# First graph aggregation on one core: the 500-column one-hot of the hot tiles moves from ACT to VectorE, and four products of a tile become one

## The chip, the core and the metric

The kernel runs on one core of a Trainium2 chip. The time is that of the device, in microseconds, from the start of one execution to its end. It is given as the median of a few executions. Beside the times there is one profiled execution, in which the hardware profiler recorded the instructions of each engine: PE (the matrix engine), DVE (VectorE), ACT (ScalarE), POOL (GpSimd) and SP (SyncE).

## The reference

A graph of 3125 nodes with 256 features and 50,000 weighted edges goes through two layers, each an aggregation over the graph and a mixture of experts. Only the first aggregation is touched here:

```python
h = layernorm(x) @ W
msgs = h[dst] * edge_weight[:, None]
x = x + segment_sum(msgs, src, 3125) + bias
```

`dst` is sorted and its values are drawn as 3125 u^2 with u uniform, so that low nodes are frequent: 500 of the 3125 nodes, the "hot" ones, receive about four tenths of the edges. All in float32.

## The kernel before

**Preparation** (`stage_prepare`, L534). The nodes are cut into 25 blocks of P = 125. Each edge gets a bucket: the block of its source, and 25 more buckets for edges whose target is hot (`dst` < HOT * P = 500, L660). The edges are put into tiles of 128 slots, tile by tile of one bucket, in `pg.slots` [128, EDGE_PAD, 4] with EDGE_PAD = 592 tiles; the last dimension holds source place in its block, weight and target, so a column of one field is strided by four floats. One part of the edges goes there by POOL's scatters to DRAM (L634), the rest by products with permutation matrices (`Permute`, L417); `unpack` (L516) and `merge` (L523, L526 to L528) end the preparation on VectorE by adding the two parts. `step` is a `Chain` (L138): VectorE waits for each such instruction before it issues the next. A `pg.block()` ends when all engines are done, so the aggregation cannot start before the last step.

**Cold tiles** (class `Aggregate`, L748). A round is 16 tiles. ACT copies the targets as integers and the keys of four tiles (`stage`, L776, L782 and L783), POOL gathers 128 rows of `h` for each tile from DRAM by an indirect DMA (`gather_round`, L801) into one of 16 places of `G`, VectorE writes the weighted one-hot of the source place, 125 columns, into `S` (`onehot`, L840), and PE multiplies two tiles into one bank (`product_four`, L826 in this stage), which VectorE adds to the rows of `pg.X` of the source block (`add`, L859). POOL may gather into a place again when PE is done with the tile of the round before.

**Hot tiles** (`stage_aggregate_nodes`, L881). Their targets are among 500 nodes, so no row is gathered: the stage builds the matrix `pg.A` [125, 4, 3125], weights by hot target (row in its block of 125, block d of four) and source node, and later multiplies it with the 500 hot rows of `h` (L1069; the three later feature layers use the same `pg.A` at L1099). A round is HR = 12 tiles, in Q = 3 quads of QUAD = 4 tiles of one source block. For each tile VectorE writes the weighted one-hot of the source place, `S`, 125 columns (`sources`, L940). ACT writes the one-hot of the target, `T`, 500 columns, with two activations: `away` = |column - target| (L926), then relu(1 - away) (L932); its keys come from `stage_hot` (L916, L917). PE makes, for each of the four target blocks d, the product of `T[:, k, d * P:(d + 1) * P]` and `S[:, k, :]`, summed over the quad's four tiles (`quad_product`, L950), and VectorE adds the bank of 500 columns to `pg.A` (`quad_add`, L960) and writes the sources of the quad's places for the next round.

**The order.** While both lists last (`both_lists`), each engine has an order written out by hand: PE takes four cold tiles, then three times a quad and four cold tiles; ACT stages four cold tiles between the targets of two quads; VectorE adds a four, adds a quad and writes the next sources. POOL's queue in this stage holds nothing but the gathers. In this run there are 16 cold rounds (256 gathers) and 17 hot ones (204 tiles, 51 quads). Before the loop VectorE writes 8 cold and 12 hot one-hots (L865, L1027), adds the bias to X (L1028) and clears `pg.A` (L1030); the first hot product waits for that (`s_add`). After the loop SP loads the hot rows (L1083) in a new block.

Of the kernel before, what the change touches and what calls it, by code (L numbers as in the profile page):

```python
# [24 lines left out]
ALU = mybir.AluOpType  # L25
ACT = mybir.ActivationFunctionType
# [4 lines left out]
P = 125  # L31
# [8 lines left out]
HOT = 4  # L40
QUAD = 4
HR = 3 * QUAD
# [6 lines left out]
EDGE_PAD = -(-(EDGE_TILES + 2 * HR) // ROUND) * ROUND  # L49
# [22 lines left out]
class Program:  # L72
# [8 lines left out]
    def sb(self, name, shape, dt=fp32, ctx=None):  # L81
        return (ctx or self.ctx).enter_context(self.nc.sbuf_tensor(name, shape, dt))
# [451 lines left out]
def stage_prepare(pg, x, src, dst, edge_weight, w_l0, bias_l0):  # L534
    nc = pg.nc
    with ExitStack() as ctx:
        sb = lambda n, s, d=fp32: pg.sb(n, s, d, ctx)
# [17 lines left out]
        perm = Permute(pg, ctx, sort_room)  # L555
# [18 lines left out]
        with pg.block() as block:  # L574
# [64 lines left out]
            def _(dve):  # L639
                step = Chain(dve, s_ch)  # L640
                v = nc.vector
# [57 lines left out]
                first, end = buf["start"][0:1, NT:NT + 1], buf["start"][0:1, EB:EB + 1]  # L699
# [13 lines left out]
                perm.unpack(step)  # L713
                dve.wait_ge(s_back, 16)
                perm.merge(step)

            @block.tensor
            def _(pe):
# [162 lines left out]
def stage_aggregate_nodes(pg):  # L881


    nc = pg.nc
    SPAN = 4
    Q = HR // QUAD
    with ExitStack() as ctx:
        agg = Aggregate(pg, ctx, "agg0", "node", pg.X)
        sb = lambda n, s, d=fp32: pg.sb(n, s, d, ctx)
        S, T = sb("hot_sources", [128, HR, P]), sb("hot_targets", [128, HR, HOT * P])  # L890
        away = sb("hot_away", [128, QUAD, HOT * P])
        key = sb("hot_key", [128, HR, 3])
        s_key, s_neg, s_away, s_src, s_dst, s_mm, s_add, s_bias = (pg.sem(f"hot_{n}", ctx) for n in (
            "key", "negated", "away", "sources", "targets", "mm", "add", "biased"))
# [14 lines left out]
        def block_psum(q):  # L909
            return pg.ps[0:P, 4 + q, 0:HOT * P].rearrange("p (d q) -> p d q", d=HOT)  # L910

        def stage_hot(act, first, i):

            act.wait_ge(s_src, i * HR + HR)
            act.wait_ge(s_dst, i * HR + HR)
            nc.scalar.copy(key[:, :, 0:2], pg.slots[:, pg.tiles_at(first + i * HR, HR), 0:2]).then_inc(s_key, 1)  # L916
            nc.scalar.activation(key[:, :, 2], pg.slots[:, pg.tiles_at(first + i * HR, HR), 2],  # L917
                                 ACT.Copy, scale=-1.0).then_inc(s_neg, 1)

        def targets(act, i, q):  # L920

            act.wait_ge(s_neg, i + 1)
            for u in range(QUAD):
                k = q * QUAD + u
                act.wait_ge(s_dst, i * HR + (k + HR - QUAD + 1))
                nc.scalar.activation(away[:, u, :], pg.hot_col[:], ACT.Abs,  # L926
                                     bias=key[:, k, 2:3]).then_inc(s_away, 1)
            act.wait_ge(s_mm, i * Q + (q + 1))
            for u in range(QUAD):
                k = q * QUAD + u  # L930
                act.wait_ge(s_away, i * HR + (k + 1))
                nc.scalar.activation(T[:, k, :], away[:, u, :], ACT.Relu, bias=pg.ones[:, 0:1],  # L932
                                     scale=-1.0).then_inc(s_dst, 1)

        def sources(dve, i, q):
            if q == 0:
                dve.wait_ge(s_key, i + 1)
            dve.wait_ge(s_mm, i * Q + (q + 1))
            for k in range(q * QUAD, (q + 1) * QUAD):
                nc.vector.tensor_scalar(S[:, k, :], pg.col[:, 0:P], key[:, k, 0:1], key[:, k, 1:2],  # L940
                                        ALU.is_equal, ALU.mult).then_inc(s_src, 1)

        def quad_product(pe, i, q):
            pe.wait_ge(s_add, i * Q + (q + 1))
            pe.wait_ge(s_src, i * HR + (HR + (q + 1) * QUAD))
            pe.wait_ge(s_dst, i * HR + (HR + (q + 1) * QUAD))
            for d in range(HOT):
                for u in range(QUAD):
                    k = q * QUAD + u
                    last = nc.tensor.matmul(block_psum(q)[:, d, :], T[:, k, d * P:(d + 1) * P], S[:, k, :],  # L950
                                            start=(u == 0), stop=(u == QUAD - 1))
            last.then_inc(s_mm, 1)

        def quad_add(dve, first, i, q):
# [8 lines left out]
        with pg.block() as block:  # L963
            @block.scalar
            def _(act):
                n, m, first = agg.rounds(act), agg.rounds(act, HOTTER), agg.rounds(act, FIRST)
                act.sem_inc(s_dst, HR)

                def both_lists(i):
                    agg.stage(act, i, 0)  # L970
                    stage_hot(act, first, i)
                    for q in range(Q):
                        agg.stage(act, i, q + 1)
                        targets(act, i, q)

                def either_list(i):


                    with act.If(n > i - 1):
                        agg.stage(act, i, 0)  # L980
                    with act.If(m > i - 1):
                        stage_hot(act, first, i)
                    with act.If(n > i - 1):
                        agg.stage(act, i, 1)
                    with act.If(n > i):
                        agg.stage(act, i, 2)
                        agg.stage(act, i, 3)
                    with act.If(m > i):
                        for q in range(Q):
                            targets(act, i, q)  # L990

                rounds_of_lists(act, both_lists, either_list)
# [987 lines left out]
def build(nc, x, src, dst, edge_weight, L0_gnn_W, L0_gnn_bias, L0_ffn_router_w, L0_ffn_w1, L0_ffn_b1,  # L1980
          L0_ffn_w2, L0_ffn_b2, L1_gnn_W_in, L1_gnn_b_in, L1_gnn_W1, L1_gnn_b1, L1_gnn_g1, L1_gnn_be1,
          L1_gnn_W2, L1_gnn_b2, L1_gnn_g_out, L1_gnn_b_out, L1_ffn_Wr, L1_ffn_W1s, L1_ffn_b1s,
          L1_ffn_W2s, L1_ffn_b2s, L1_ffn_W1p, L1_ffn_b1p, L1_ffn_W2p, L1_ffn_b2p, out):
    with ExitStack() as ctx:
        pg = Program(nc, ctx)
        pg.ps = ctx.enter_context(nc.psum_tensor("ps", [128, 8, 512], fp32))
        pg.X = pg.sb("X", [P, NT, D])
        pg.stats = pg.sb("stats", [P, NT, 6])
        pg.col = pg.sb("col", [128, 128])
        pg.part = pg.sb("part", [128, 1])  # L1990
        pg.moe_tiles = pg.sb("moe_tiles", [1, MOE_TILES])
        pg.ident = pg.sb("ident", [128, 128])
        pg.tri = pg.sb("tri", [128, 128])
        pg.ones = pg.sb("ones", [128, 128])
        pg.prio = pg.sb("prio", [P, NX])
        pg.token = pg.sb("token", [P, TOP * NT])
        pg.H = nc.dram_tensor("h_rows", [N, D], fp32).ap()
        pg.pay_dram = nc.dram_tensor("payloads", [128 * EDGE_PAD, 4], fp32).ap()
        pg.Y = nc.dram_tensor("expert_out", [MOE_TILES * SLOT, D], fp32).ap()

        edges = ctx.enter_context(ExitStack())
        pg.slots = pg.sb("slots", [128, EDGE_PAD, 4], ctx=edges)
        pg.owner_t = pg.sb("owner_t", [1, EDGE_PAIRS], int32, ctx=edges)
        pg.owner_n = pg.sb("owner_n", [1, EDGE_PAIRS], int32, ctx=edges)
        pg.owner_h = pg.sb("owner_h", [1, EDGE_PAIRS], int32, ctx=edges)
        pg.lists = pg.sb("lists", [1, 6], int32, ctx=edges)
        pg.tiles = pg.sb("tiles", [1, EDGE_PAIRS], ctx=edges)
        pg.bias_l0 = pg.sb("bias_l0", [P, D], ctx=edges)
        pg.hot_col = pg.sb("hot_col", [128, HOT * P], ctx=edges)
        stage_prepare(pg, x, src, dst, edge_weight, L0_gnn_W, L0_gnn_bias)  # L2010
        pg.A = pg.sb("A_hot", [P, HOT, N], ctx=edges)
        stage_aggregate_nodes(pg)
        with ExitStack() as c1:
            Mixture(pg, c1, "moe0", lambda k: L0_ffn_router_w.rearrange("e (k p) -> k p e", p=128)[k],
                    L0_ffn_w1, L0_ffn_b1, L0_ffn_w2, L0_ffn_b2).run()
        stage_network(pg, L1_gnn_W_in, L1_gnn_b_in, L1_gnn_W1, L1_gnn_b1, L1_gnn_g1, L1_gnn_be1,
                      L1_gnn_W2, L1_gnn_b2, L1_gnn_g_out, L1_gnn_b_out)
        edges.close()

        with ExitStack() as c1:  # L2020
            Mixture(pg, c1, "moe1", lambda k: L1_ffn_Wr[k * 128:(k + 1) * 128, :],
                    L1_ffn_W1p, L1_ffn_b1p, L1_ffn_W2p, L1_ffn_b2p,
                    shared=(L1_ffn_W1s, L1_ffn_b1s, L1_ffn_W2s, L1_ffn_b2s), out=out).run()
# [30 lines left out]
```

## Time and profile before

| | us |
|---|---|
| median of 3 executions | 3124.06 (3123.24 to 3125.66) |
| the profiled execution | 3120.67 |
| its span in the profile | 3118.9 |
| PE busy | 2358.3 (76% of the span) |
| POOL busy | 1466.8 (47%) |
| DVE busy | 1362.2 (44%) |
| ACT busy | 947.9 (30%) |
| first aggregation's loop, first to last hot instruction | 437.5 to 789.5 |

Busy times are shares of the whole span, over stages with different limits; matmuls are pipelined, so a busy PE is not PE at its peak. An engine's idle time is put down to what released it: "ACT agg_key L783" is the semaphore of that line, "issue" is time in which it waited for nothing that the profile shows. A group's count and busy time belong to the instructions of one line, and its mean is that of one instruction from start to end, which is more than the step between two that overlap.

### The profile page before, as it was taken

How to read it: one execution, taken by the hardware profiler on the slowest of the kernel's cores; microseconds unless marked ns; L12 is line 12 of the kernel's file. 1: busy time of each engine (PE TensorE's matmuls, PEld its weight loads, DVE VectorE, ACT ScalarE, POOL GpSimd, SP SyncE). 2: the span in 40 equal slices, each digit the busy share in tenths (PEclk: the TensorE clock that was granted, in tenths of full speed). 3: DMA queues.
4: the chain of work that ended last, by engine and by line, in shares of the span. 5: the costliest groups of instructions: out<-in, count | busy, mean ns of one | idle time of the engine just before them, and what ended most of it. 6: DMA issues, size and time to landing. Idle time of an engine off the chain costs nothing. (4 is left out here: it accounts for less than half of the span.)

```text
span 3118.9 us, 52528 instructions
## 1 busy us (share of the span) xinstructions
PE 2358.3 (76%) x13838; PEld 2087.4 (67%) x13838; DVE 1362.2 (44%) x3807; ACT 947.9 (30%) x2741; POOL 1466.8 (47%) x1443
## 2 busy tenths in 40 slices
PE   1989959999769615667575676656665799999999
PEld 0789959888668503666535665436564499999988
DVE  6789976666344352434333434234343541111122
ACT  4268858788012101000040000220000433333332
POOL 1388867776004452777606777227776001111152
PEclk9889979999859857888787888778987879999999
DMA  2100013333019732333303333123333049999932
GB/s 78 35 4 3 3 47 100 104 104 93 21 65 322 242 86 76 105 104 104 90 23 108 104 104 105 36 80 104 104 105 86 11 128 308 326 329 325 326 94 64
DMA packets 250553, 363.11 MB, mean 116 GB/s; under 512 B 64305, under 2 KB 195854, under 8 KB 250054
## 3 DMA queue, kind: packets, MB, share of 16 engines
q0 software_dynamic: 73728, 163.66, 19.3%
q1 hardware_dynamic: 173460, 194.84, 19.1%
q10 hardware_dynamic: 3250, 3.20, 0.3%
q8 instruction: 58, 0.95, 0.1%
q14 instruction: 57, 0.47, 0.0%
HBM read 322.19 MB, written 38.64 MB: 116 GB/s over the span
## 5 line engine op out<-in xcount | busy, mean ns | idle before, releaser
L801 POOL DMA_INDIRECT z_or_xn<-h_rows,agg_idx x768 | 730.3, 951 | 524.5 <-ACT agg_key L783 301.2
L832 PE MATMUL ps<-z_or_xn 128*128 128x125 f32 x3072 | 496.1, 328 | 325.0 <-DMA z_or_xn<-h_rows,agg_idx 281.2
L832 PEld LDWEIGHTS ps<-z_or_xn 128*128 128x128 f32 x3072 | 461.5, 237 | 363.9 <-issue 284.9
L1410 POOL DMA_INDIRECT moe_room<-h_rows,moe_inverse x112 | 105.8, 944 | 725.4 <-PE ps L1491 390.4
L859 DVE TENSOR_TENSOR z<-z,ps 128x250 f32 x384 | 159.3, 415 | 543.7 <-PE ps L832 510.3
L782 ACT CAST agg_idx<-slots 128x4 int32 x264 | 51.8, 196 | 1056.2 <-PE ps L832 605.9
L634 POOL DMA_INDIRECT payloads<-pay_st,idx_st x176 | 247.7, 1407 | 159.7 <-DMA idx_st<-slot_i 106.3
L801 POOL DMA_INDIRECT agg_room<-h_rows,agg_idx x256 | 249.1, 973 | 97.6 <-issue 70.2
L1610 ACT ACTIVATE moe_room<-ps,moe_b 128x128 f32<-128x128 f32 x560 | 163.6, 367 | 364.0 <-PE ps L1503 363.9
L502 PE MATMUL ps<-perm_tile,perm_weighted 125*128 125x296 f32 x1792 | 247.5, 301 | 9.7 <-ACT perm_weighted L489 9.7
L502 PEld LDWEIGHTS ps<-perm_tile,perm_weighted 125*128 125x128 f32 x1792 | 247.2, 190 | 10.6 <-ACT perm_weighted L489 10.6
L840 DVE TENSOR_SCALAR z_or_xn<-col,agg_key 128x125 f32<-128x125 f32 x792 | 241.1, 367 | 19.9 <-ACT agg_key L783 19.9
L489 ACT ACTIVATE perm_weighted<-oh_or_permute 125x128 fp32r<-125x128 f32 x672 | 206.1, 390 | 111.3 <-DVE oh_or_permute L473 111.2
L1636 DVE TENSOR_TENSOR moe_room<-ps,moe_b 128x256 f32<-128x256 f32 x112 | 47.5, 424 | 431.1 <-PE ps L1515 431.1
L1099 PE MATMUL ps<-A_hot,agg_hot_rows 125*128 (+1 forms) x624 | 174.1, 434 | 61.7 <-DMA agg_hot_rows<-h_rows 61.7
L950 PEld LDWEIGHTS ps<-hot_sources,hot_targets 128*125 128x125 f32 x1632 | 189.9, 192 | 18.4 <-issue 15.2
L950 PE MATMUL ps<-hot_sources,hot_targets 128*125 128x125 f32 x1632 | 189.9, 275 | 14.1 <-DVE A_hot L1030 13.6
L1099 PEld LDWEIGHTS ps<-A_hot,agg_hot_rows 125*128 125x128 f32 x624 | 139.6, 244 | 79.5 <-DMA agg_hot_rows<-h_rows 62.6
L1503 PE MATMUL ps<-moe_room,moe_w_ring 128*128 128x128 f32 x1520 | 185.6, 278 | 2.8 <-issue 2.0
L1503 PEld LDWEIGHTS ps<-moe_room,moe_w_ring 128*128 128x128 f32 x1520 | 177.5, 193 | 6.5 <-issue 4.1
L1515 PE MATMUL ps<-moe_w_ring,moe_room 128*128 128x256 f32 x760 | 177.2, 380 | 2.7 <-issue 2.7
L1420 POOL DMA_INDIRECT moe_room<-expert_out,moe_slot_i x100 | 120.8, 1208 | 94.7 <-DMA expert_out<-moe_room 58.3
(272 smaller groups left out, 3572.2 us busy)
## 6 DMA issues: line engine op xcount, KB each, us to landing
moe_w_ring<-in_L_ffn_W1p_dram SPq DMA_DIRECT2D x38, 1024.0 KB, 7.0
moe_w_ring<-in_L_ffn_W2p_dram SPq DMA_DIRECT2D x38, 1024.0 KB, 7.9
moe_w_ring<-in_L_ffn_w_dram SPq DMA_DIRECT2D x76, 256.0 KB, 5.0
moe_room<-in_L_ffn_W1p_dram SPq DMA_DIRECT2D x18, 1024.0 KB, 7.1
moe_room<-in_L_ffn_W2p_dram SPq DMA_DIRECT2D x18, 1024.0 KB, 7.7
expert_out<-moe_room SPq DMA_DIRECT2D x112, 128.0 KB, 5.7
z_or_xn<-h_rows,agg_idx POOLq DMA_INDIRECT x768, 2.7
moe_room<-in_L_ffn_w_dram SPq DMA_DIRECT2D x36, 256.0 KB, 4.7
```

Source lines behind the costliest of these rows:

```text
L489: last = self.pg.nc.scalar.activation(self.weighted[:, u, x, :], self.place[:, u, :], ACT.Copy, scale=self.parts[:, bass.ds(i * long + c, ...
L502: last = nc.tensor.matmul(self.ps[:, x // 2, h, :], self.weighted[:, u, x, :], self.tile[:, u, h * (EDGE_PAD // 2):(h + 1) * (EDGE_PAD // 2)],
L634: g.indirect_dma_start(pg.pay_dram, bass.IndirectOffsetOnAxis(ap=idx_st[:, h, k:k + 1], axis=0), pay_st[:, h, k, :], None).then_inc(scat[8 ...
L801: self.pg.nc.gpsimd.indirect_dma_start(self.G[:, k, :], None, self.pg.H, bass.IndirectOffsetOnAxis(ap=self.idx[:, k:k + 1], axis=0)).then_ ...
L832: last = nc.tensor.matmul(out[:, c, :], self.G[:, k, c * 128:(c + 1) * 128], self.S[:, k, :], start=(u == 0), stop=(u == PAIR - 1))
L840: self.pg.nc.vector.tensor_scalar(self.S[:, k, :], self.pg.col[:, 0:P], self.key[:, k, 0:1], self.key[:, k, 1:2], ALU.is_equal, ALU.mult). ...
L859: nc.vector.tensor_tensor(a, a, p, ALU.add).then_inc(self.s_acc, 1)
L950: last = nc.tensor.matmul(block_psum(q)[:, d, :], T[:, k, d * P:(d + 1) * P], S[:, k, :], start=(u == 0), stop=(u == QUAD - 1))
L1099: last = nc.tensor.matmul(pg.ps[:, 4 + c, 0:width], Hh[:, d, c * 128:(c + 1) * 128], pg.A[:, d, bass.ds(first, width)], start=(d == 0), st ...
L1503: last = nc.tensor.matmul(self.fc1_psum(t, f), w[:, k, f * 128:(f + 1) * 128], self.xt[:, t % self.RT, k, :], start=(k == 0), stop=(k == K ...
L1515: last = nc.tensor.matmul(ps[:, 6 + t % 2, 0:D], self.hid[:, t % self.RH, f, :], w[:, f, :], start=(f == 0), stop=(f == FK - 1))
L1610: last = a.activation(self.hid[:, t % self.RH, f, :], self.fc1_psum(t, f), ACT.Gelu, bias=self.b1_sb[:, bass.ds(e, 1), f])
```

## The change

The two one-hots swap their widths. VectorE's weighted one-hot now spans 500 columns, target block and source place together, and stands as the moving operand; ACT's one-hot of the target's row in its block has 125 columns and is the weight. One product a tile gives the whole bank of 500 columns. For this the keys of all tiles are worked out once, behind `merge`: `pg.hot_key[:, :, 1]` is the target's row in its block, `pg.hot_key[:, :, 0]` the source place plus 125 times the block. `row_of` and `block_of` count minus 125 for each block's start that the target has reached.

```diff
@@ stage_prepare, VectorE, behind perm.merge(step)
+                block_of, dst_of = perm.got_i[:, 0, :], pg.slots[:, :, 2]
+                key_of, row_of = pg.hot_key[:, :, 0], pg.hot_key[:, :, 1]
+                step(v.tensor_scalar(row_of, dst_of, float(P), -float(P), ALU.is_ge, ALU.mult))
+                for d in range(2, HOT):
+                    step(v.tensor_scalar(block_of, dst_of, float(d * P), -float(P), ALU.is_ge, ALU.mult))
+                    step(v.tensor_tensor(row_of, row_of, block_of, ALU.add))
+                step(v.tensor_tensor(key_of, pg.slots[:, :, 0], row_of, ALU.subtract))
+                step(v.tensor_tensor(row_of, dst_of, row_of, ALU.add))
@@ stage_aggregate_nodes
-        S, T = sb("hot_sources", [128, HR, P]), sb("hot_targets", [128, HR, HOT * P])
-        away = sb("hot_away", [128, QUAD, HOT * P])
+        S, T = sb("hot_sources", [128, HR, HOT * P]), sb("hot_targets", [128, HR, P])
+        away = sb("hot_away", [128, QUAD, P])
@@ stage_hot, ACT
-            nc.scalar.copy(key[:, :, 0:2], pg.slots[:, pg.tiles_at(first + i * HR, HR), 0:2]).then_inc(s_key, 1)
-            nc.scalar.activation(key[:, :, 2], pg.slots[:, pg.tiles_at(first + i * HR, HR), 2],
+            nc.scalar.copy(key[:, :, 1], pg.slots[:, pg.tiles_at(first + i * HR, HR), 1])
+            nc.scalar.copy(key[:, :, 0], pg.hot_key[:, pg.tiles_at(first + i * HR, HR), 0]).then_inc(s_key, 1)
+            nc.scalar.activation(key[:, :, 2], pg.hot_key[:, pg.tiles_at(first + i * HR, HR), 1],
                                  ACT.Copy, scale=-1.0).then_inc(s_neg, 1)
@@ targets, ACT
-                nc.scalar.activation(away[:, u, :], pg.hot_col[:], ACT.Abs,
+                nc.scalar.activation(away[:, u, :], pg.col[:, 0:P], ACT.Abs,
@@ sources, VectorE
-                nc.vector.tensor_scalar(S[:, k, :], pg.col[:, 0:P], key[:, k, 0:1], key[:, k, 1:2],
+                nc.vector.tensor_scalar(S[:, k, :], pg.hot_col[:], key[:, k, 0:1], key[:, k, 1:2],
@@ quad_product, PE
-            for d in range(HOT):
-                for u in range(QUAD):
-                    k = q * QUAD + u
-                    last = nc.tensor.matmul(block_psum(q)[:, d, :], T[:, k, d * P:(d + 1) * P], S[:, k, :],
-                                            start=(u == 0), stop=(u == QUAD - 1))
+            for u in range(QUAD):
+                k = q * QUAD + u
+                last = nc.tensor.matmul(pg.ps[0:P, 4 + q, 0:HOT * P], T[:, k, :], S[:, k, :],
+                                        start=(u == 0), stop=(u == QUAD - 1))
@@ build
+        pg.hot_key = pg.sb("hot_keys", [128, EDGE_PAD, 2], ctx=edges)
```

## Rows read from the trace of the kernel before

**Rows 1.** Busy time by stretch: PE, PEld, DVE, ACT, POOL, granted clock, DMA share, GB/s.

```profile
463.00:470.00 7.00, 7.00 (x43) 6.78 (x43) 1.91 (x7) 0.00 (x0) 4.80 (x5) 0.76 0.34 100
503.30:769.20 265.90, 246.44 (x1747) 228.82 (x1746) 168.90 (x531) 218.21 (x464) 201.48 (x212) 0.97 0.36 104
520.00:540.00 20.00, 20.00 (x150) 18.95 (x149) 14.58 (x46) 18.59 (x39) 15.13 (x17) 1.00 0.36 105
```

**Rows 2.** Groups, 503.3 to 769.2 (the last row: whole span); columns as on the page.

```profile
L801 POOL DMA_INDIRECT agg_room<-h_rows,agg_idx x212 | 201.5, 950 | 64.8 <-issue 57.0 <-ACT agg_key L783 6.7 <-PE ps L826 1.1
...
L826 PE MATMUL ps<-agg_room 128*125 128x256 f32 x435 | 109.1, 397 | 19.5 <-DMA agg_room<-h_rows,agg_idx 16.1 <-DVE X L859 2.2 <-DVE agg_room L840 1.1
...
L960 DVE TENSOR_TENSOR A_hot<-A_hot,ps 125x500 f32 x51 | 34.5, 676 | 20.4 <-issue 15.3 <-PE ps L950 4.8
```

**Rows 3.** Groups, POOL, 1230 to 1520 (a feature layer).

```profile
L801 POOL DMA_INDIRECT z_or_xn<-h_rows,agg_idx x232 | 220.9, 952 | 70.7 <-issue 67.0 <-ACT agg_key L783 3.7
```

**Rows 4.** Timeline, POOL: start, us, line, what, [idle before and its releaser].

```profile
438.39 1.06 POOL L801 DMA_INDIRECT agg_room<-h_rows,agg_idx  x1 [15.92 <-ACT agg_key L783]
...
439.76 1.02 POOL L801 DMA_INDIRECT agg_room<-h_rows,agg_idx  x1 [0.30 <-issue]
...
443.61 6.62 POOL L801 DMA_INDIRECT agg_room<-h_rows,agg_idx  x1 [0.30 <-ACT agg_key L783]
...
471.25 0.95 POOL L801 DMA_INDIRECT agg_room<-h_rows,agg_idx  x1 [2.21 <-ACT agg_key L783]
```

**Rows 5.** Timeline, 439 to 468, DVE and PE.

```profile
439.53 3.14 DVE L940 TENSOR_SCALAR hot_sources<-col,hot_key 128x125 f32<-128x125 f32 x12
...
442.59 6.81 DVE L1028 TENSOR_TENSOR X<-X,bias_l 125x6400 f32<-125x6400 f32 x1
...
451.95 10.47 DVE L1030 MEMSET A_hot<- 125x12500 f32 x1 [2.56 <-issue]
...
462.67 5.48 PE L950 MATMUL ps<-hot_sources,hot_targets 128*125 128x125 f32 x32 [13.62 <-DVE A_hot L1030]
```

**Rows 6.** Groups, POOL, 471.2 to 503.3.

```profile
L801 POOL DMA_INDIRECT agg_room<-h_rows,agg_idx x24 | 22.8, 948 | 11.1 <-issue 7.8 <-ACT agg_key L783 3.3
```

**Rows 7.** Timeline, ACT: half a quad's activations of 500 columns, and four of 128.

```profile
603.44 2.52 ACT L926 ACTIVATE hot_away<-hot_col,hot_key 128x500 f32<-128x500 f32 x4
...
2601.94 1.14 ACT L1610 ACTIVATE moe_room<-ps,moe_b 128x128 f32<-128x128 f32 x4 [0.45 <-PE ps L1503]
```

**Rows 8.** Timeline, PE: a dense layer from 1175.54 on, the tail's three quads.

```profile
1175.54 16.64 PE L1790 MATMUL ps<-h_features,gnn_w 128*128 128x500 f32 x43
...
776.97 10.71 PE L950 MATMUL ps<-hot_sources,hot_targets 128*125 128x125 f32 x96 [0.49 <-ACT hot_targets L932]
```

**Rows 9.** Timeline, DVE, end of the preparation (merge).

```profile
429.30 1.21 DVE L526 TENSOR_TENSOR slots<-slots,oh_or_permute 128x592 f32<-128x592 f32 x1 [1.44 <-DMA slots<-payloads]
...
431.78 1.23 DVE L528 TENSOR_TENSOR slots<-slots,oh_or_permute 128x592 f32<-128x592 f32 x1
```

**Rows 10.** One line each: count, shortest/median/longest ns, first and last start, shape.

```profile
L652 DVE TENSOR_SCALAR slot_i<-src_f x1: 368/368/368, 10.6 to 10.6; 125x400 int32<-125x400 f32 x1
...
L660 DVE TENSOR_SCALAR row_f<-pay x1: 511/511/511, 14.5 to 14.5; 125x400 f32<-125x400 f32 x1
```

**Rows 11.** The same view: one-hot, two-operation tensor_scalar, wide tensor_scalar.

```profile
L840 DVE TENSOR_SCALAR agg_room<-col,agg_key x264: 330/341/549, 437.5 to 777.2; 128x125 f32<-128x125 f32 x132
...
L1703 DVE TENSOR_SCALAR moe_xn<-X,moe_mean,moe_rstd x50: 398/405/412, 852.6 to 2500.2; 125x256 f32<-125x256 f32 x50
...
L475 DVE TENSOR_SCALAR perm_tile<-tile_row,slot_f x224: 512/523/865, 176.2 to 420.9; 125x592 fp32r<-125x592 f32 x112
```

**Rows 12.** L634: before the permutation (one line), beside it (group).

```profile
L634 POOL DMA_INDIRECT payloads<-pay_st,idx_st x14: 1172/1177/4312, 121.4 to 144.0; - x14
...
L634 POOL DMA_INDIRECT payloads<-pay_st,idx_st x154 | 205.0, 1331 | 46.9 <-issue 46.9
```

**Rows 13.** The line L801, whole span.

```profile
L801 POOL DMA_INDIRECT agg_room<-h_rows,agg_idx x256: 940/946/6615, 438.4 to 768.2; - x128
```

## The prediction

> **What bounds the kernel now.** I looked first at busy times by stretch [rows 1]. In the first aggregation, between 503 and 769 us, no engine is full: PE is busy 246.4 of 265.9 us, ACT 218.2, POOL 201.5, DVE 168.9. So the waits must tell, and I took the groups of that stretch [rows 2]. POOL issues 212 gathers there (L801), 950 ns each, with 64.8 us idle before them, 0.306 us each: 212 x 1.256 = 266 us is the whole stretch. Is that 0.30 a wait for ACT's keys, which the row partly names? The same gather in a feature layer, where no hot tile is built, comes at the same step: 232 in (220.9 + 70.7) us, 1.257 each [rows 3]. So the step is POOL's own, and POOL is the loop's clock: a round is 16 gathers, 20 us. PE (L826) stops 16.1 us for gathers to land [rows 2]. ACT, the engine that the change relieves most, is busy 18.6 of 20 us [rows 1], yet behind POOL.
>
> Only the beginning is different. POOL stops before the gather at 471.25 (idle 2.21) [rows 4]: the first hot product must wait until DVE has cleared A_hot, at 451.95 + 10.47 us, so that PE resumes at 462.67 [rows 5]. From there to 503 us POOL is idle 11.1 us before 24 gathers [rows 6], 3.9 more than 24 x 0.30. In this catch-up ACT needs 2 x 2.52 us for the eight activations of a quad of hot tiles, and its key copies on top [rows 7]; four gathers take 5.0, so POOL meets ACT and PE at their own pace.
>
> **The change, part by part.** The sum is made against the profiled execution, 3120.67 us with a span of 3118.9; that lies 3.4 us under the median 3124.06, and I add the sum to the median.
>
> *ACT.* A quad's eight activations of 500 columns (four in 2.52 us) become eight of 125; four of 128 columns take 1.14 us [rows 7]. ACT saves 2.7 us a quad, some 138 us over 51 quads, and gains one key copy a round. By itself this is worth nothing: POOL's step hides it. It pays where ACT ends last, in the catch-up and by 0.5 us at the tail.
>
> *PE.* A quad is 32 matmul instructions now (the trace lists two to an fp32 product); the tail's three quads, 96 of them, take 10.71 us, 3.6 a quad. After, it is 8 of 500 columns. 43 instructions of a dense layer, nearly all 500 wide, took 16.64 us, 0.39 apart, so 0.42 for the wide ones [rows 8]: 3.4 a quad. That saves 0.2, again behind POOL. PE will stand longer for gathers, so its clock may dip more often: after the stop of 13.62 us before 462.67 the granted clock of the next 7 us was 0.76 of full [rows 1], a mean of the levels 1.2 and 2.4 GHz, and the quad took 5.48 [rows 5], 1.9 more. I cost such dips at nothing, since PE's waits for gathers cover them; without that cover one a round would be 1.9 x 16 = 30 us.
>
> *Seven new VectorE steps.* They stand at the very end of the preparation, chained behind merge (L526 to L528). DVE is done at 431.78 + 1.23 = 433.0 [rows 9], and POOL, idle for 15.92 us, starts its first gather 5.4 us later [rows 4]. Nothing lies beside them: all of it is on the path. Four are tensor_tensor on strided operands like the three of merge, whose step is (431.78 - 429.30) / 2 = 1.24 us with the gap: 5.0. Three are tensor_scalar: striding cost L660 0.14 over L652 for 400 columns [rows 10], so 0.21 for 592, on top of 0.52 for 592 contiguous ones (L475 [rows 11]): 0.73 each, 2.2. Sum **+7.2**. Below, contiguous prices: 0.52 three times and 0.80 four times (L960's 676 ns for 500 columns [rows 2]), 4.8. Above: 1.24 seven times, 8.7. I take the strided rows, since the new operands are strided.
>
> *VectorE's one-hot, 125 to 500 columns.* No row has this shape. The same two-operation form takes 341 ns at 125 columns and 405 at 256, 0.49 ns a column; the one-operation form takes 523 at 592 [rows 11]. So about 0.52, **0.18 more each**. Ahead of the loop twelve stand in front of the bias add and the clearing of A_hot (3.14 us [rows 5]), on the path to the restart at 471.25: **+2.2**, up to 3.3 if each is held up by another 0.09, as one-hots reach 549 where the median is 341. In the loop DVE gains 2.2 us on 12.7 a round; POOL's 20 covers it.
>
> *Catch-up.* ACT's quad halves, PE's shrinks by 0.2: **-1.0** of the 3.9 (0 to -2.1; the rest belongs to the restart itself).
>
> *POOL's gathers beside a wider VectorE instruction.* This decides the size. That the two hinder each other stands in the start: the gather at 443.61 took 6.62 us while the bias add ran to 449.4, and the one at 439.76, amid twelve one-hots, took 1.02 [rows 4, 5]. The nearest rows for wide instructions are the scatters L634: 1177 ns median before the permutation, 1331 mean beside it [rows 12], +154 ns, where DVE runs one instruction of 592 and two of 128 columns every 1.08 us or so. If a gather waits out the rest of the running instruction, the cost goes with the sum of squared widths per us: in the permutation 354 thousand, in the loop now 28 x 125^2 / 20 = 22 thousand, after (16 x 125^2 + 12 x 500^2) / 20 = 162 thousand. That predicts 154 x 22/354 = 10 ns for today; measured are a mean of 950 [rows 2] over a shortest of 940 [rows 13], so the form holds. After: 71, 61 more. Against the median of 946 today's loss is only 4 ns, which scales to 29, 25 more. I take the middle, 43 ns x 236 gathers from 471 us on: **+10.1**. Below: 0 (POOL slips between; nothing in the change could speed a gather). Above: 61 x 236 = 14.4.
>
> The Trainium skill, "SBUF — State Buffer", § Who interferes with whom, speaks against this change: a VectorE instruction in a 2-port mode, which it says a tensor_scalar can enter, holds a port pair that GpSimd shares for its whole length, and whichever comes second is fully blocked. The scatters' 154 ns agree that a running neighbour costs time; what the rule would make of four such instructions in a row is rival 3.
>
> *Tail.* After the last cold product PE has three quads and 0.49 us of waiting for ACT [rows 8]: -0.49 and 3 x -0.2. The four one-hots behind the last add, which nobody reads, still hold the block's end: 4 x 0.18 = +0.7. Sum **-0.4**.
>
> All: 7.2 + 2.2 - 1.0 + 10.1 - 0.4 = **+18.1**: 3138.8 for the profiled execution, **3142.2** by the median.
>
> **The rivals.** (1) *ACT paces the loop.* For it: ACT's 18.6 of 20 us, and its key copies named as releaser before L801. Against it: 1.257 us a gather where ACT has next to nothing to do [rows 3]. If the 0.30 us before each gather were ACT's, the round would fall to PE's 246.4 / 265.9 x 20 = 18.5 us: 16 x 1.5 = 24 less, against 8.0 more outside the loop: 3108. It decides if a round gets shorter than 20 us. Chance 0.05. (2) *POOL is not disturbed* and the new steps are at their low price: 4.8 + 2.2 - 2.1 - 0.4 = +4.5, 3129; L801 stays at 950 ns. Chance 0.12. (3) *A quad's four one-hots shut POOL out as one*: 4 x 0.46 = 1.8 us, a mean wait of 0.9, 48 times: +43 in place of 10.1, 3175. Against it: twelve one-hots without a gap lengthened a gather to no more than 1.02 [rows 4, 5]. Chance 0.04. (4) *The wide one-hot runs at the price of the 500-column add*, 676 ns [rows 2]: +0.34 each, 4.0 at the start and 1.3 at the tail, and POOL perhaps left alone: 7.2 + 4.0 - 1.0 + 0.2 = +10.4, 3134. DVE would be at 16.7 of 20 us, still no bound. Chance 0.07.
>
> **How the numbers follow.** Forecast 0.72, rivals 0.05, 0.12, 0.04, 0.07. A measurement of this kernel tells about 0.2% from no change, 6.2 us, so slower means over 3130.3: rivals 3 and 4 and nearly all of the forecast, 0.82. Rival 2 and a low forecast are the same, 0.13. Faster is rival 1, 0.05. Lowest sum 4.8 + 2.2 - 2.1 + 0 - 0.4 = +4.5; highest 8.7 + 3.3 + 0 + 14.4 + 0 = +26.4. So the range is 3128 to 3151; rivals 1 and 3 stay outside.
>
> **What would show it.** Right: seven DVE instructions behind L528 of some 7 us together, and the first gather later by as much; one-hots of about 0.52 us in hot_sources; ACT about half busy in the loop; PE waiting more for gathers; L801 near 0.99 us with 0.30 before it, so a round above 20 us. Wrong: L801 still at 0.95 (rival 2), a round under 20 us (rival 1), gathers of 1.5 us and more at each quad (rival 3), one-hots of 0.65 us and more (rival 4).

## The result, and the profile after

The changed kernel takes **3142.01 us** (median of 4 runs, 3137.07 to 3145.01) against 3123.76 (3123.24 to 3125.66) beside it: ratio **1.0056**, 95% interval 1.0038 to 1.0073. That is slower, as forecast, and 0.2 us from the forecast time. The profiled execution took 3137.07 us with a span of 3135.2; the span of before is 3118.9, so 16.3 us are to be found in the trace.

First the timeline of after (start, us, engine, line, what, [idle before and its releaser]): VectorE at the end of the preparation and at the loop's start, POOL's first gathers, ACT in the loop, and PE and VectorE at the tail.

```profile
432.66 0.70 DVE L718 TENSOR_SCALAR hot_keys<-slots 128x592 f32<-128x592 f32 x1
433.39 0.68 DVE L720 TENSOR_SCALAR oh_or_permute<-slots 128x592 int32<-128x592 f32 x1
434.11 0.78 DVE L721 TENSOR_TENSOR hot_keys<-hot_keys,oh_or_permute 128x592 f32<-128x592 f32 x1
...
437.70 1.22 DVE L723 TENSOR_TENSOR hot_keys<-slots,hot_keys 128x592 f32<-128x592 f32 x1
...
445.45 5.48 DVE L949 TENSOR_SCALAR hot_sources<-hot_col,hot_key 128x500 f32<-128x500 f32 x12
450.85 6.81 DVE L1036 TENSOR_TENSOR X<-X,bias_l 125x6400 f32<-125x6400 f32 x1
460.21 10.47 DVE L1038 MEMSET A_hot<- 125x12500 f32 x1 [2.55 <-issue]
...
444.31 1.06 POOL L809 DMA_INDIRECT agg_room<-h_rows,agg_idx  x1 [22.22 <-ACT agg_key L791]
445.68 12.83 POOL L809 DMA_INDIRECT agg_room<-h_rows,agg_idx  x1 [0.30 <-issue]
458.81 0.94 POOL L809 DMA_INDIRECT agg_room<-h_rows,agg_idx  x1 [0.30 <-issue]
...
481.35 1.23 POOL L809 DMA_INDIRECT agg_room<-h_rows,agg_idx  x1 [0.30 <-issue]
...
606.46 1.26 ACT L935 ACTIVATE hot_away<-col,hot_key 128x125 f32<-128x125 f32 x4
607.63 1.25 ACT L941 ACTIVATE hot_targets<-hot_away,ones 128x125 f32<-128x125 f32 x4
...
783.99 3.52 PE L958 MATMUL ps<-hot_sources,hot_targets 128*125 128x500 f32 x8
...
791.37 10.30 PE L958 MATMUL ps<-hot_sources,hot_targets 128*125 128x500 f32 x24 [0.48 <-issue]
817.46 7.87 PE L1077 MATMUL ps<-hot_rows,A_hot 125*125 125x256 f32 x28 [15.79 <-DMA hot_rows<-h_rows]
...
802.40 1.88 DVE L949 TENSOR_SCALAR hot_sources<-hot_col,hot_key 128x500 f32<-128x500 f32 x4
```

Against [rows 4, 5, 7 to 9]: the seven steps run from 432.66 to 438.92, 6.26 us, and the first gather starts 5.92 later than before (merge itself began 0.35 earlier here). The second gather is the new thing: it takes 12.83 us, from inside the twelve one-hots until just after the bias add has ended at 450.85 + 6.81 = 457.66. In the kernel before, the one long gather was the fifth, 6.62 us beside the bias add. So late is POOL afterwards that A_hot is ready when the 21st gather is due: it starts at 481.35 without a stop, where before had 2.21 us of idle time at 471.25. An activation quad takes 2.5 us in place of 5.0.

Then the loop: busy time of 20 us (PE, PEld, DVE, ACT, POOL, granted clock, DMA share, GB/s), and two groups of the stretch 509.6 to 783.3, the last 214 gathers.

```profile
520.00:540.00 20.00, 18.32 (x59) 10.65 (x58) 15.75 (x42) 9.26 (x37) 15.16 (x16) 1.00 0.36 104
```

```profile
L809 POOL DMA_INDIRECT agg_room<-h_rows,agg_idx x214 | 209.6, 979 | 65.2 <-issue 60.6 <-ACT agg_key L791 4.6
...
L834 PE MATMUL ps<-agg_room 128*125 128x256 f32 x429 | 110.6, 404 | 30.3 <-DMA agg_room<-h_rows,agg_idx 28.2 <-DVE agg_room L848 2.0
```

Beside [rows 1, 2]: ACT falls from 18.59 us to 9.26, PE from 20.00 to 18.32, DVE rises from 14.58 to 15.75. A gather's mean goes from 950 ns to 979 with the same 0.305 us before it, so the round is longer, and PE waits for gathers 28.2 us where it waited 16.1. The same by line (count, shortest/median/longest ns, first and last start):

```profile
L809 POOL DMA_INDIRECT agg_room<-h_rows,agg_idx x256: 942/946/12831, 444.3 to 783.0; - x128
...
L949 DVE TENSOR_SCALAR hot_sources<-hot_col,hot_key x216: 520/534/767, 445.4 to 803.8; 128x500 f32<-128x500 f32 x108
```

The median gather is still 946 ns [rows 13]. The mean moved because 21 gathers behind the start took 1.14 to 1.24 us and about as many 1.02; of those behind the start, none took over 1.06 before. One of the 21, with the one-hot that was running when it started:

```profile
520.69 0.52 DVE L949 TENSOR_SCALAR hot_sources<-hot_col,hot_key 128x500 f32<-128x500 f32 x1
520.83 1.20 POOL L809 DMA_INDIRECT agg_room<-h_rows,agg_idx  x1 [0.30 <-issue]
```

The one-hot ends at 521.21, the gather at 522.03, 0.82 us later. So it is with all 21: each starts 0.12 to 0.21 us after a one-hot has started and ends 0.81 to 0.82 us after that one-hot's end, just as in the kernel before the 6.62 us gather ended 0.82 us after the bias add. An undisturbed gather takes 0.95 us in all. But not every neighbour costs time: of 73 gathers behind the start that started while a one-hot was running, 25 took less than 0.96 us.

A ledger for what follows, worked out from the starts and lengths of the 256 gathers in the trace: 255 gaps of 1.25 us (0.95 and 0.30) is the shortest way from the first gather's start to the last's. What lies above that is lost, either in long gathers among the first eight, in gathers from the ninth on, or in POOL's idle time above 0.30 us. The parts count from a median gather of 946 ns and add up to the sum within 0.2 us.

| profiled execution | lost, us | first eight | later gathers | idle | mean from the ninth on, ns |
|---|---|---|---|---|---|
| before | 11.1 | 5.9 | 1.0 | 4.1 | 950 |
| after | 19.9 | 12.0 | 7.8 | 0.1 | 978 |
| keys_alone | 11.1 | 5.9 | 0.9 | 4.3 | 950 |
| wide_alone | 21.9 | 12.0 | 10.0 | 0.1 | 986 |
| halves | 15.1 | 7.4 | 2.3 | 5.4 | 955 |
| psum_col (long gather is the ninth) | 14.1 | 0.1 | 7.0 | 6.9 | 974 |
| after_again | 22.2 | 12.0 | 10.0 | 0.2 | 986 |
| bias_later_after | 14.4 | 5.3 | 9.2 | 0.1 | 983 |
| bias_later_before | 3.9 | 0.2 | 0.8 | 2.9 | 949 |
| bias_later_psum | 7.1 | 0.2 | 0.7 | 6.2 | 949 |
| clear_first_before | 15.3 | 13.1 | 2.1 | 0.2 | 954 |
| clear_first_after | 23.7 | 13.9 | 9.7 | 0.2 | 985 |
| clear_first_halves | 17.0 | 13.2 | 3.6 | 0.2 | 961 |

For the span of after: 5.9 later first gather, 8.9 more to the last gather (338.69 from the first gather's start to the last's, where before took 329.81), 0.0 at the tail (21.3 us from the last gather's start to VectorE's end in both), 14.8 in all. The other 1.5 us come later, where no instruction is changed, and are spread; runs of this kernel differ by up to 7.9.

### The profile page after: what moved, and what is told of

The parts are those of the page before. It is cut to its first block and busy times, and to the rows that moved or that the text cites. A ratio compares the mean times of both kernels' runs of the same rounds, so it can differ in the third digit from the quotient of the medians.

```text
span 3135.2 us, 50123 instructions
## 1 busy us (share of the span) xinstructions
PE 2352.4 (75%) x12614; PEld 1976.4 (63%) x12614; DVE 1414.3 (45%) x3814; ACT 821.5 (26%) x2759; POOL 1478.8 (47%) x1443
## 5 line engine op out<-in xcount | busy, mean ns | idle before, releaser
L634 POOL DMA_INDIRECT payloads<-pay_st,idx_st x176 | 247.4, 1405 | 159.6 <-DMA idx_st<-slot_i 106.3
L809 POOL DMA_INDIRECT agg_room<-h_rows,agg_idx x256 | 262.0, 1023 | 99.9 <-issue 72.5
L848 DVE TENSOR_SCALAR z_or_xn<-col,agg_key 128x125 f32<-128x125 f32 x792 | 240.8, 365 | 20.1 <-ACT agg_key L791 19.9
L958 PE MATMUL ps<-hot_sources,hot_targets 128*125 128x500 f32 x408 | 184.7, 597 | 4.7 <-DVE A_hot L1038 4.2
L834 PE MATMUL ps<-agg_room 128*125 128x256 f32 x512 | 131.8, 404 | 70.1 <-DMA agg_room<-h_rows,agg_idx 68.0
L834 PEld LDWEIGHTS ps<-agg_room 128*125 128x125 f32 x512 | 98.7, 198 | 114.8 <-issue 96.0
```

Source lines behind the costliest of these rows:

```text
L634: g.indirect_dma_start(pg.pay_dram, bass.IndirectOffsetOnAxis(ap=idx_st[:, h, k:k + 1], axis=0), pay_st[:, h, k, :], None).then_inc(scat[8 ...
L809: self.pg.nc.gpsimd.indirect_dma_start(self.G[:, k, :], None, self.pg.H, bass.IndirectOffsetOnAxis(ap=self.idx[:, k:k + 1], axis=0)).then_ ...
L834: last = nc.tensor.matmul(out, self.S[:, k, :], self.G[:, k, :], start=(u == 0), stop=(u == PAIR - 1))
L848: self.pg.nc.vector.tensor_scalar(self.S[:, k, :], self.pg.col[:, 0:P], self.key[:, k, 0:1], self.key[:, k, 1:2], ALU.is_equal, ALU.mult). ...
L958: last = nc.tensor.matmul(pg.ps[0:P, 4 + q, 0:HOT * P], T[:, k, :], S[:, k, :], start=(u == 0), stop=(u == QUAD - 1))
```

## The experiments

**Which parts make the 18 us?** My theory: the seven steps cost some 6 us, and the rest is the wide one-hot, which holds gathers up, at the start and in the loop. Its rival: the new order on ACT and PE matters (one product a tile, ACT's short rows). Two kernels do one part each. *keys_alone* is before with the seven steps, whose result nobody reads:

```diff
                 perm.merge(step)
+                block_of, dst_of = perm.got_i[:, 0, :], pg.slots[:, :, 2]
+                key_of, row_of = pg.hot_key[:, :, 0], pg.hot_key[:, :, 1]
+                step(v.tensor_scalar(row_of, dst_of, float(P), -float(P), ALU.is_ge, ALU.mult))
...
+                step(v.tensor_tensor(row_of, dst_of, row_of, ALU.add))
```

> The kernel before plus the seven VectorE steps behind merge; nothing reads their tile. Theory L (the new time is these steps plus gathers that wait for wide VectorE one-hots): +6.3 us, the 6.26 us that the steps take in the changed kernel, since nothing lies beside them; about 3130. Loop, gathers and start as before. Rival P (the steps are hidden by the change of blocks): +2 or less.

Measured: 3127.68 us, ratio 1.0012 (1.0003 to 1.0022) to 3121.44 of before on its chip: **+6.2**. Its row of the ledger is that of before, so a late start is all there is.

*wide_alone* is before with one-hots 500 wide, of which the products read the first 125 columns, so that the answer stays the same:

```diff
-        S, T = sb("hot_sources", [128, HR, P]), sb("hot_targets", [128, HR, HOT * P])
+        S, T = sb("hot_sources", [128, HR, HOT * P]), sb("hot_targets", [128, HR, HOT * P])
...
-                nc.vector.tensor_scalar(S[:, k, :], pg.col[:, 0:P], key[:, k, 0:1], key[:, k, 1:2],
+                nc.vector.tensor_scalar(S[:, k, :], pg.hot_col[:], key[:, k, 0:1], key[:, k, 1:2],
...
-                    last = nc.tensor.matmul(block_psum(q)[:, d, :], T[:, k, d * P:(d + 1) * P], S[:, k, :],
+                    last = nc.tensor.matmul(block_psum(q)[:, d, :], T[:, k, d * P:(d + 1) * P], S[:, k, 0:P],
```

> The kernel before, with VectorE's hot one-hot written 500 columns wide; the products read its first 125 columns, ACT and PE work as before, no new steps. Theory L: the second gather is held until the one-hots and the bias add are through, about 12.8 us, and the loop's gathers take 0.97 to 1.00 us in the mean: +9 to +13 us, 3133 to 3137. Rival P (only VectorE's own chain gets longer, gathers stay at 0.95 us, the restart behind the clearing of A_hot comes 2.3 us later): +2 to +3 us, 3126.

Measured: 3132.90 us, 1.0037 (1.0025 to 1.0049), **+11.5**. Its timeline, POOL and then DVE:

```profile
439.09 12.83 POOL L801 DMA_INDIRECT agg_room<-h_rows,agg_idx  x1 [0.30 <-issue]
...
474.80 1.21 POOL L801 DMA_INDIRECT agg_room<-h_rows,agg_idx  x1 [0.30 <-issue]
...
438.86 5.49 DVE L940 TENSOR_SCALAR hot_sources<-hot_col,hot_key 128x500 f32<-128x500 f32 x12
444.26 6.82 DVE L1028 TENSOR_TENSOR X<-X,bias_l 125x6400 f32<-125x6400 f32 x1
```

The 12.83 us of the second gather and the loop's 986 ns are there with ACT and PE as they were. 6.2 + 11.5 = 17.7; the changed kernel, run again as *after_again*, came out +17.4. So ACT's halved work and PE's wide product are worth nothing that intervals of 3 to 4 us either way can show, and the rival falls as an account of the 18 us.

> The changed kernel itself, beside the kernels of this call. The sum of its two parts run alone is 6.2 + 11.5 = +17.7 us over the kernel before; if they simply add (L), +16 to +19 us. If the freed ACT and the shorter product give something back together with them, +12 or less. The second gather again 12.8 us, the later ones 975 to 985 ns in the mean.

Measured: 3139.59 us to 3122.19, 1.0056 (1.0044 to 1.0068).

**Does the length of the single instruction count?** *halves* builds each one-hot of the changed kernel in two instructions of 250 columns:

```diff
-                nc.vector.tensor_scalar(S[:, k, :], pg.hot_col[:], key[:, k, 0:1], key[:, k, 1:2],
-                                        ALU.is_equal, ALU.mult).then_inc(s_src, 1)
+                for h in range(2):
+                    half = slice(h * (HOT * P // 2), (h + 1) * (HOT * P // 2))
+                    last = nc.vector.tensor_scalar(S[:, k, half], pg.hot_col[:, half], key[:, k, 0:1], key[:, k, 1:2],
+                                                   ALU.is_equal, ALU.mult)
+                last.then_inc(s_src, 1)
```

> The changed kernel with each 500-column one-hot written as two of 250. If a gather waits out the rest of the running instruction (L), the sum of squared widths falls from 162 to 88 thousand a us and the loop's excess over 946 ns to about half of the changed kernel's 28 ns; if a burst shuts POOL out as a whole, it stays or grows with the burst. VectorE needs about 0.15 us more a tile, 1.8 us more ahead of the loop. L: 3138 to 3142. Burst as a whole: 3144 to 3150.

Measured: 3131.28 us, 1.0028 (1.0017 to 1.0038), +9.8, below the range of either theory. Timeline:

```profile
449.81 1.15 POOL L809 DMA_INDIRECT agg_room<-h_rows,agg_idx  x1 [0.30 <-issue]
...
458.17 7.35 POOL L809 DMA_INDIRECT agg_room<-h_rows,agg_idx  x1 [0.30 <-issue]
...
486.17 0.94 POOL L809 DMA_INDIRECT agg_room<-h_rows,agg_idx  x1 [5.59 <-ACT agg_key L791]
...
449.58 8.39 DVE L951 TENSOR_SCALAR hot_sources<-hot_col,hot_key 128x250 f32<-128x250 f32 x24
457.89 6.81 DVE L1039 TENSOR_TENSOR X<-X,bias_l 125x6400 f32<-125x6400 f32 x1
```

More instructions and more VectorE time (8.39 for 5.48 us), yet gathers slip in between: 1.15 and then 1.07 us amid the twenty-four. In the loop the loss falls from 7.8 or 10.0 us to 2.3. Halving divides it by three or four, steeper than the square of the width would (two): what is lost goes with the length of one instruction, not with VectorE's busy time. Whether any long instruction costs as much is asked next. The long gather is back at the bias add, and, since A_hot is now cleared late, POOL stops 5.59 us at the 21st.

**Is it VectorE's way to SBUF?** *psum_col* reads the comparison row from PSUM, so that no one-hot reads a wide operand from SBUF:

```diff
+                nc.vector.tensor_copy(pg.ps[:, 7, 0:HOT * P], pg.hot_col[:]).then_inc(s_col, 1)
+                dve.wait_ge(s_col, 1)
...
-                nc.vector.tensor_scalar(S[:, k, :], pg.hot_col[:], key[:, k, 0:1], key[:, k, 1:2],
+                nc.vector.tensor_scalar(S[:, k, :], pg.ps[:, 7, 0:HOT * P], key[:, k, 0:1], key[:, k, 1:2],
```

> The changed kernel, where VectorE's 500-column one-hot reads the column numbers from a free PSUM bank in place of SBUF (copied there once, 0.7 us). Theory L: no gather waits for a one-hot, so the loop's mean is 946 to 952 ns as before and the second gather waits for the bias add alone, 6 to 7 us, although a one-hot now takes 0.6 to 0.7 us and 12 of them 7 us or more ahead of the loop: 3130 to 3136. Rival P (VectorE's length is what costs): 3146 or more.

Measured: 3132.07 us, 1.0032 (1.0021 to 1.0042), +10.6. Timeline, the last two lines from the loop:

```profile
445.01 0.97 POOL L809 DMA_INDIRECT agg_room<-h_rows,agg_idx  x1 [0.30 <-issue]
...
453.78 7.11 POOL L809 DMA_INDIRECT agg_room<-h_rows,agg_idx  x1 [0.30 <-issue]
...
481.63 0.94 POOL L809 DMA_INDIRECT agg_room<-h_rows,agg_idx  x1 [6.93 <-ACT agg_key L791]
...
453.25 6.81 DVE L1038 TENSOR_TENSOR X<-X,bias_l 125x6400 f32<-125x6400 f32 x1
...
528.24 0.95 POOL L809 DMA_INDIRECT agg_room<-h_rows,agg_idx  x1 [0.30 <-issue]
...
528.24 2.91 DVE L949 TENSOR_SCALAR hot_sources<-ps,hot_key 128x500 f32<-128x500 f32 x4
```

The one-hots are longer (791 ns median for 534), and no gather is held by them: 0.97 amid the twelve, 0.95 for one that starts with a burst of four. Behind the start 108 gathers begin while such a one-hot runs, and every one takes less than 0.96 us. A longer instruction that hinders nobody: this settles for the loop that neither the length of a one-hot nor VectorE's busy time holds a gather by itself, but a one-hot that reads its wide operand from SBUF. The Trainium skill, "SBUF — State Buffer", § Who interferes with whom, says that a VectorE instruction outside the 2-port modes with at most one SBUF input doesn't contend with GpSimd, while a tensor_scalar in such a mode does; the run agrees (0.95 us beside PSUM one-hots, up to 1.24 beside SBUF ones), though no trace shows which mode an instruction ran in. A PSUM one-hot also runs at a slower pace, 0.71 us apart in a row for 0.46, and no run tells that apart from the operand's place. The time is no better than that of *halves*: the twelve one-hots ahead of the clearing of A_hot take 8.56 us for 5.48, POOL stops 6.93 us for it, and the tail is 1.7 us longer.

**What is the bias add worth?** It held a gather 6.6 to 7.4 us in before, *halves* and *psum_col*. Three kernels add the bias at the head of the next block, where VectorE has nothing to do until the first share product:

```diff
-                nc.vector.tensor_tensor(pg.X[:], pg.X[:], pg.bias_l0[:].unsqueeze(1).to_broadcast([P, NT, D]),
-                                        ALU.add).then_inc(s_bias, 1)
                 nc.vector.memset(pg.A[:], 0.0).then_inc(s_add, Q)
-                dve.wait_ge(s_bias, 1)
...
             def _(dve):
+                nc.vector.tensor_tensor(pg.X[:], pg.X[:], pg.bias_l0[:].unsqueeze(1).to_broadcast([P, NT, D]),
+                                        ALU.add).then_inc(s_bias, 1)
+                dve.wait_ge(s_bias, 1)
                 for j in range(NT):
```

> The changed kernel with the bias add at the head of the next block, where VectorE waits some 17 us for the hot rows. L: the second gather is held by the twelve one-hots alone, about 6 us in place of 12.8, and as A_hot is cleared 9 us earlier no wait takes its place: 6 to 7 us less than the changed kernel, +10 to +12 over the kernel before; the loop's gathers stay at 975 to 985 ns. Rival: the start is hidden behind the clearing of A_hot, as the prediction had it: 9 us less, and the gather's length does not matter.

Measured: 3132.64 us, 1.0039 (1.0026 to 1.0052): 7.0 less than after_again. Timeline:

```profile
444.22 6.10 POOL L809 DMA_INDIRECT agg_room<-h_rows,agg_idx  x1 [0.30 <-issue]
...
443.98 5.48 DVE L949 TENSOR_SCALAR hot_sources<-hot_col,hot_key 128x500 f32<-128x500 f32 x12
452.02 10.47 DVE L1036 MEMSET A_hot<- 125x12500 f32 x1 [2.55 <-issue]
```

Of the 12.83 us, 6.73 were the bias add and the rest the twelve one-hots: the gather ends 0.86 us after the last of them, so it was shut out by all of them together.

> The kernel before with the bias add at the head of the next block. L: no gather above 1.1 us, A_hot clear 9.4 us earlier, so POOL does not stop at the 21st gather and runs at 1.25 us a gather from the first to the last: of 11.1 us lost between them 8 to 9.5 go, 3112 to 3114 where the kernel before has 3121. Rival (the start is hidden, or the add shows again in the next block): within 3 us of the kernel before.

Measured: **3115.48 us, 0.9978 (0.9967 to 0.9988)**: 6.7 us faster than the kernel before, and the best version here. By line, and VectorE's timeline in the next block:

```profile
L801 POOL DMA_INDIRECT agg_room<-h_rows,agg_idx x256: 942/946/1072, 442.6 to 765.2; - x128
```

```profile
793.32 6.82 DVE L1072 TENSOR_TENSOR X<-X,bias_l 125x6400 f32<-125x6400 f32 x1 [7.32 <-PEq L114]
803.83 0.42 DVE L1077 TENSOR_TENSOR X<-X,ps 125x256 f32<-125x256 f32 x1 [3.69 <-PE ps L1066]
```

No gather takes over 1.07 us, and the moved add is hidden: VectorE is done with it at 800.14 and still waits 3.69 us for PE. The gain falls short of the 8 to 9.5 us expected, since POOL does stop at the 21st gather and loses 2.9 us of idle time from there on:

```profile
468.77 0.94 POOL L801 DMA_INDIRECT agg_room<-h_rows,agg_idx  x1 [1.29 <-ACT agg_key L783]
```

> The changed kernel with the column numbers in PSUM and the bias add in the next block: no VectorE instruction holds a gather up any more, all at 0.95 us. What is left over the kernel before is the 6.3 us of the seven steps and, since twelve one-hots take 8.6 us ahead of the clearing of A_hot, a stop of some 4 us at the 21st gather, against the 11.1 us that the kernel before loses: -1 to +3 us.

Measured: 3128.33 us, 1.0019 (1.0009 to 1.0029), +6.1: a miss. No gather is held, as expected, but the expectation left out that a POOL that isn't held reaches the clearing of A_hot sooner: it stops 6.22 us before the 21st gather. The steps' 6.2, 4.0 less lost than before (7.1 for 11.1) and a tail 1.7 us longer, with its PSUM one-hots, make 3.9 of the 6.1; the rest is not found, and the interval is 3.1 us either way.

```profile
479.71 0.94 POOL L809 DMA_INDIRECT agg_room<-h_rows,agg_idx  x1 [6.22 <-ACT agg_key L791]
```

**Can both waits go?** Gathers run at 0.95 us beside the clearing of A_hot in before and after, so I put the clearing first and the one-hots behind it, with the bias later, in three kernels:

```diff
+                nc.vector.memset(pg.A[:], 0.0).then_inc(s_add, Q)
                 for q in range(Q):
                     sources(dve, 0, q)
-                nc.vector.memset(pg.A[:], 0.0).then_inc(s_add, Q)
```

> The kernel before with the bias add in the next block and A_hot cleared ahead of the twelve hot one-hots. The first hot product needs four of them behind the clearing, so PE starts it some 2 us earlier than with the bias moved alone; the stop at the 21st gather (1.0 us above 0.30) and part of the 1.9 us lost in the catch-up go: 1 to 2.5 us less than with the bias moved alone, 8 to 10 less than the kernel before, 3112 to 3114 where that has 3122. Rival: PE, cold after its wait, paces the catch-up as before, and nothing changes.

Measured: 3131.20 us to 3124.47, 1.0021 (1.0012 to 1.0030): +6.7 where a gain was expected.

```profile
438.77 13.80 POOL L801 DMA_INDIRECT agg_room<-h_rows,agg_idx  x1 [0.30 <-issue]
...
436.49 2.13 DVE L840 TENSOR_SCALAR agg_room<-col,agg_key 128x125 f32<-128x125 f32 x8 [4.48 <-ACT agg_key L783]
441.18 10.47 DVE L1026 MEMSET A_hot<- 125x12500 f32 x1 [2.55 <-issue]
```

The second gather starts at 438.77, when VectorE shows nothing (in every kernel some 2.55 us without a record stand ahead of the clearing), 2.4 us ahead of the memset's record, and ends 0.92 after it. Its 13.80 us take back more than the moved bias add gives.

> The changed kernel with the same two moves. The burst of twelve 500-column one-hots now comes 10.5 us later and meets another gather. If such a burst always shuts POOL out to its end, one gather of up to 6.4 us stands there, and the time is that of the changed kernel with the bias moved, about 10 us over the kernel before; if POOL gets in between two of them, as in the loop, no gather is over 1.3 us: 5 us less, about +5.

Measured: 3144.57 us, 1.0071 (1.0057 to 1.0084): +20.1, a miss.

```profile
447.93 13.99 POOL L809 DMA_INDIRECT agg_room<-h_rows,agg_idx  x1 [0.31 <-issue]
462.23 1.19 POOL L809 DMA_INDIRECT agg_room<-h_rows,agg_idx  x1 [0.30 <-issue]
...
460.73 5.95 DVE L949 TENSOR_SCALAR hot_sources<-hot_col,hot_key 128x500 f32<-128x500 f32 x12
```

Again the second gather pays, this time for the clearing; the third then gets in amid the very twelve one-hots that shut a gather out in after, for 0.25 us.

> The changed kernel in halves of 250 columns with the same two moves: gathers slip between (1.1 us at most), the loop's mean is 955 ns, and the seven steps' 6.3 us stand against the start's 8 to 10 us: -2 to +2 us against the kernel before. It would be the least that this way of building A_hot costs; if it is slower than the kernel before with the same moves by about 6 to 8 us, the freed ACT gives nothing back.

Measured: 3138.89 us, 1.0044 (1.0030 to 1.0057), +14.4, a miss too; second gather 13.86 us, later mean 961 ns. The idea fails in all three, and why the second gather is held so long stays **open**.

## Why the prediction was right, point by point

- **Seven steps** (forecast 7.2): 6.26. The step that was off is "four are tensor_tensor on strided operands": the two that read the new tile and the contiguous scratch tile take 0.78, not 1.24, while the two that read slots take 1.22; the three tensor_scalar take 0.69 where I had 0.73. keys_alone's +6.2 confirms the whole.
- **The start** (+2.2 and -1.0 for the catch-up): the net was near, +6.1 for long gathers and -4.0 for idle time, 2.1 for a forecast of 1.2, but the mechanism was another. "On the path to the restart at 471.25" is the step that failed: POOL was delayed past that restart by a gather shut out for the whole run of one-hots and bias add, and the catch-up vanished with it. That the net came near is luck. Rival 3 described this and I gave it little, since the twelve one-hots of 125 columns lengthened a gather to 1.02 at most; that row didn't carry over to 500 columns. In the loop rival 3 is wrong: no gather there took over 1.24 us beside bursts of four.
- **POOL's gathers** (forecast +43 ns each, 10.1 us): 27 ns, 6.8 us in the profiled execution, 36 ns in after_again and wide_alone, 9.0 us in each. That lies between the two scalings I had (25 and 61); the 43 was only their middle. The form "a gather waits out the rest of the running instruction" is what the loop's slow gathers do, each of the 21 in after ending 0.81 to 0.82 us after its one-hot, but as a rule of cost it holds in part: *psum_col* limits it to one-hots that read SBUF, *halves* falls more steeply than the squares, and it works in few and whole steps: 21 to 30 gathers lose about 0.25 us each, and most of the others little or nothing. At the start it fails. With the loop's loss rival 2 (POOL undisturbed) is out.
- **The one-hot** (0.52): 534 ns median, 0.46 apart in a row. Twelve took 5.48 us against 3.14, +2.3 for +2.2. Rival 4 (0.68) is out.
- **ACT and PE**: ACT is half busy in the loop and PE's quad takes 3.52 for 3.4, both worth nothing; ACT's four activations took 1.26, not 1.14. wide_alone with the old ACT and PE loses as much. What the catch-up was to give (-1.0, at most -2.1) may show in *halves*, *psum_col* and bias_later_psum, which do stop at the 21st gather: POOL is never idle over 0.4 us behind it there, where before lost 2.1 us in six more stops and bias_later_before 1.8 in five. Whether ACT's shorter quad, PE's product or the longer stop does that, no run separates. Rival 1 (ACT paces) is out: no round got shorter. PE's waits in the loop grew by 12.1 us, and its granted clock from 520 to 540 us stayed at 1.00.
- **Tail** (-0.4): 0.0. Its three quads began 0.4 earlier behind the last gather, won another 0.4 and the last one-hots lost 0.8, [rows 8] against 791.37 and 802.40 here. The 0.49 us of waiting that I took off is still there, 0.48, though no longer put down to ACT.
- **Sum**: to VectorE's end 14.8 where I had 18.1, in an execution that is 4.9 us under its median; after_again, near its own, lost 22.2 - 11.1 = 11.1 us between first and last gather, and with the 6.2 of the steps that is 17.3 of the 17.4 measured. The closeness of 3142.2 to 3142.0 owes something to errors that offset each other.

## What to carry to other kernels

Before widening an instruction on an engine with slack, ask who shares its way to memory with the engine that sets the pace: here VectorE had 5 us in 20 to spare and the kernel still lost 9 to 11 us, because POOL's gathers stood behind it. Taking work from an engine that isn't the clock (ACT, 18.6 to 9.3 us a round) bought nothing. And a long VectorE instruction beside a stream of POOL gathers is worth moving to a place where no gather is under way: the bias add, moved one block on, gave 6.7 us by itself, though its own time was hidden anyway. Such a move has to be measured: with the clearing of A_hot moved as well, the kernel came out 6.7 us slower than before.

## What the runs showed of the hardware that was not expected

- A gather that came second to a row of back-to-back VectorE instructions was let in after the whole row at the start (12.83 us over twelve one-hots and a tensor_tensor; 6.10 over the one-hots alone), but after the running one in the loop (1.14 to 1.24 us), and in clear_first_after amid the same twelve (1.19). What distinguishes the cases isn't known; all of the first kind are the second gather after POOL's long pause.
- The clearing of A_hot held that second gather for 13.8 to 14.0 us when it came right behind VectorE's first eight one-hots (three kernels; the gather ended 0.84 us after the first one-hot behind the clearing), and none when it came later (0.95 us each in before and after).
- The bias add, a tensor_tensor with two SBUF operands, made one gather last 6.6 to 7.4 us in every kernel where it ran beside them and none was held already. The Trainium skill, "SBUF — State Buffer", § Who interferes with whom, says that such an instruction contends with GpSimd's reads of SBUF, but also that a probe didn't see it stall DMA, for which it infers that making descriptors needs only the write side. The runs show that an indirect gather waits for it (6.62 us in before); that the reading of its index list agg_idx is the reason is not shown.
- The operand's place sets the one-hot's time: 534 ns from SBUF, 791 from PSUM, 404 for 250 columns from SBUF.
